# The last tile of every image moved from TensorE's transposes to GpSimd's split and DMA transposes, in a non-local attention kernel

## The reference

```python
g     = (einsum('bchw,oc->bhwo', x, w_g)     + b_g).reshape(B, N, Ci)      # N = 1024, Ci = 64
theta = (einsum('bchw,oc->bhwo', x, w_theta) + b_theta).reshape(B, N, Ci)
phi   = (einsum('bchw,oc->bohw', x, w_phi)   + b_phi[:, None, None]).reshape(B, Ci, N)
att   = softmax(einsum('bnc,bcm->bnm', theta, phi), axis=-1)
y     = einsum('bnm,bmc->bnc', att, g).reshape(B, H, W, Ci)
out   = einsum('bhwc,oc->bohw', y, w_out) + b_out[:, None, None]
inv   = bn_gamma / sqrt(bn_var + 1e-5)
return x + out * inv[:, None, None] + (bn_beta - bn_mean * inv)[:, None, None]
```

## Time and profile before

| | |
|---|---|
| median of 3 runs | 215.8 us (214.25 to 217.01) |
| the profiled execution, time | 214.18 us |
| its span on the core | 212.4 us |
| PE busy | 202.0 us, 95% |
| DVE busy | 181.7 us, 86% |
| ACT busy | 143.4 us, 68% |
| POOL busy | 130.6 us, 61% |
| TensorE clock granted | 1.0 of full speed all through |
| DMA queue of SP | 63.7% of the 16 engines' span |

### The profile page before, as it was taken

One profiled execution on the slowest core, in us unless ns is written; L12 is line 12 of the kernel. 1 busy time (PEld: TensorE's weight loads), 2 busy tenths in 40 slices (PEclk: granted clock), 3 DMA queues, 4 the chain that ended last, 5 costly groups with the idle time before them and its releaser, 6 DMA issues.

```text
span 212.4 us, 4045 instructions
## 1 busy us (share of the span) xinstructions
PE 202.0 (95%) x1156; PEld 137.4 (65%) x1156; DVE 181.7 (86%) x298; ACT 143.4 (68%) x259; POOL 130.6 (61%) x113
## 2 busy tenths in 40 slices
PE   7997969999999999999999999999999999999994
PEld 6685838576665857577575956668575855656542
DVE  0689987987999799977999599977999789989871
ACT  2777857668585848866596666856696585758721
POOL 2449786848489494866679494885769352913400
PEclk9999999999999999999999999999999999999999
DMA  5225991699529974599819994299924994182102
GB/s 159 83 76 109 210 225 27 174 221 238 114 78 241 245 182 99 126 209 250 158 50 218 243 217 113 87 223 251 167 63 105 222 235 104 38 195 49 49 11 91
DMA packets 44716, 31.61 MB, mean 149 GB/s; under 512 B 35616, under 2 KB 36128, under 8 KB 44704
## 3 DMA queue, kind: packets, MB, share of 16 engines
q1 hardware_dynamic: 44416, 31.34, 63.7%
q10 hardware_dynamic: 288, 0.14, 0.2%
HBM read 8.36 MB, written 4.23 MB: 59 GB/s over the span
## 4 chain that ended last, share of the span: by engine, by line
PE 61%; DVE 14%; issue 8%; ACT 6%; DMA 4%; SPq 3%; POOL 2%; ACTq 1%; DVEq 0%
PE ps_scores L713 18%; PE ps_flip L778 13%; PE ps_y L725 10%; PE ps_misc L697 5%; DVE pt_lo L678 5%; PE ps_y L732 5%; DVE neg_max L579 5%; PE ps_misc L803 4%; PE ps_misc L739 4%; ACT probs L537 3%; DVE y_norm L596 2%; DMA phi_ll<-lo 2%; DMA vec<-vectors_dram 2%; SPq L286 2%; ACT pt_hi L525 2%
## 5 line engine op out<-in xcount | busy, mean ns | idle before, releaser
L537 ACT ACTIVATE probs<-ps_scores,neg_max 128x1024 f32<-128x1024 f32 x64 | 71.7, 1121 | 22.5 <-DVE neg_max L579 22.4
L579 DVE TENSOR_REDUCE neg_max<-ps_scores 128x1 f32<-128x1024 f32 x64 | 77.8, 1215 | 1.2 <-PE ps_scores L713 1.2
L678 DVE SCALAR_TENSOR_TENSOR pt_lo<-ps_flip,pt_hi 128x512 f16<-128x512 f32 x98 | 62.9, 684 | 15.3 <-ACT pt_hi L525 15.1
L525 ACT ACTIVATE pt_hi<-ps_flip 128x512 f16<-128x512 f32 x98 | 53.4, 597 | 26.5 <-PE ps_flip L778 26.5
L778 PE MATMUL ps_flip<-ident,probs 128*128 128x128 f32 x392 | 52.7, 276 | 1.1 <-DVE pt_lo L678 0.6
L778 PEld LDWEIGHTS ps_flip<-ident,probs 128*128 128x128 f32 x392 | 43.6, 142 | 13.8 <-issue 6.1
L713 PE MATMUL ps_scores<-phi_hh,theta_hl 128*128 128x512 f32 x128 | 45.7, 438 | 3.8 <-DMA phi_ll<-lo 1.8
L713 PE MATMUL ps_scores<-phi_ll,theta_hl 128*128 128x512 f32 x128 | 40.0, 393 | 0.0
L406 POOL TENSOR_TENSOR p_lo<-probs,p_hi 128x1024 f16<-128x1024 f32 x15 | 32.3, 2155 | 2.9 <-POOL p_hi L402 2.3
L725 PE MATMUL ps_y<-pt_hi,g_parts 128*128 128x512 f16 (+1 forms) x128 | 30.0, 377 | 0.0
L713 PEld LDWEIGHTS ps_scores<-phi_hh,theta_hl 128*128 128x128 f32 x128 | 19.3, 190 | 14.9 <-ACT probs L537 12.2
(11 more groups left out here) (80 smaller groups left out, 179.3 us busy)
## 6 DMA issues: line engine op xcount, KB each, us to landing
x_in<-x_in_dram SPq DMA_DIRECT2D x16, 256.0 KB, 3.2
inv_all<-inv_row SPq DMA_DIRECT2D x15, 256.0 KB, 3.7
out_dram<-resid SPq DMA_DIRECT2D x15, 256.0 KB, 3.1
phi_hh<-hi SPq DMA_DIRECT2D x14, 256.0 KB, 4.9
phi_ll<-lo SPq DMA_DIRECT2D x14, 256.0 KB, 4.1
theta_hl<-hi SPq DMA_DIRECT2D x7, 256.0 KB, 4.0
theta_hl<-lo SPq DMA_DIRECT2D x7, 256.0 KB, 3.8
pt_hi<-p_hi SPq DMA_TRANSPOSE x15, 3.6
```

The lines of the kernel that those rows point to most:

```text
L525: nc.scalar.activation(pt_hi[ring][:, c * HALF_TILES:(c + 1) * HALF_TILES, slot * P:(slot + 1) * P], ps_flip[c][:, :].rearrange("p (a n) - ...
L537: nc.scalar.activation(probs[k % PROB_RING][:, :], ps_scores[k % 2][:, :], ACT.Exp, bias=neg_max[:, k % STEPS:k % STEPS + 1], accum_out=ro ...
L579: nc.vector.tensor_reduce(out=top, in_=ps_scores[k % 2][:, :], op=ALU.max, axis=AX.X, negate=True).then_inc(row_max_ready if by_dma(it, k) ...
L678: nc.vector.scalar_tensor_tensor(out=pt_lo[ring][where], in0=ps_flip[c][:, :].rearrange("p (a n) -> p a n", n=P), scalar=PROB_SCALE, in1=p ...
```

## The change

`BY_DMA` now lists places in an image (0 to 7) and not slots of a half, and place 7 is added: tiles 1, 5 and 7 go by DMA. For that the counts of flips and moves, and the semaphore values that follow from them, are made by image. The buffers `p_hi` and `p_lo` are now one pair for each of the three places (before: one pair for each half). SP's list gets the two transposes of the last tile of the image before, one ahead of the store and one behind it. The last tile of the last image still goes by TensorE, so seven tiles move.

```diff
-    BY_DMA = (1,)
-    BY_PE = tuple(slot for slot in range(HALF_TILES) if slot not in BY_DMA)
-    MOVED = 16 * len(BY_DMA)
+    BY_DMA = (1, 5, 7)
+    BY_PE = tuple(place for place in range(MT) if place not in BY_DMA)
+    IN_HALF = tuple(tuple(place % HALF_TILES for place in BY_DMA if place // HALF_TILES == part)
+                    for part in range(PER_IMAGE))
...
-        p_hi = [[sbuf(f"p_hi{i}{s}", [P, N], F16) for s in BY_DMA] for i in range(2)]
-        p_lo = [[sbuf(f"p_lo{i}{s}", [P, N], F16) for s in BY_DMA] for i in range(2)]
+        p_hi = {place: sbuf(f"p_hi{place}", [P, N], F16) for place in BY_DMA}
+        p_lo = {place: sbuf(f"p_lo{place}", [P, N], F16) for place in BY_DMA}
...
         def by_dma(it, k):
-            return k % HALF_TILES in BY_DMA and not in_last_half(tile_at(it, k))
+            return k % MT in BY_DMA and not in_last_half(tile_at(it, k))
+
+        def counted(it, k, places):
+            before = sum(place < k % MT for place in places)
+            return it * (STEPS // MT * len(places)) + k // MT * len(places) + before
...
+        def moved_each(k):
+            return 16 * len(IN_HALF[ring_of(k)])
 
         def moved_by(it, k):
-            return it * (STEPS // HALF_TILES // 2 * MOVED) + (k // HALF_TILES // 2 + 1) * MOVED
+            return it * (STEPS // MT * moved_each(k)) + (k // MT + 1) * moved_each(k)
...
                 b, r = image_at(it, k), (k // MT) % 2
                 inv_to_row(2 * b - 1)
+                turn_hi(MT * b - 1)
                 store(it, k - 2 * MT + HALF_TILES)
+                turn_lo(MT * b - 1)
                 if exists(b + 2, B):
                     sp.wait_ge(g_ready, b + 1)
                     sp.wait_ge(resid_ready, b + 1)
                     load_x(b + 2, r)
...
                 if exists(t, TILES) and by_dma(it, k - 1):
-                    ring, n = ring_of(k - 1), BY_DMA.index((k - 1) % HALF_TILES)
-                    p, high, low = probs[(k - 1) % PROB_RING], p_hi[ring][n], p_lo[ring][n]
+                    ring = ring_of(k - 1)
+                    p, high, low = probs[(k - 1) % PROB_RING], p_hi[(k - 1) % MT], p_lo[(k - 1) % MT]
                     hold(probs_ready, t + 1)
-                    hold(hi_moved[ring], moved_by(it, k - 1) - MOVED)
+                    hold(hi_moved[ring], moved_by(it, k - 1) - moved_each(k - 1))
```

More of the change, by code:

```diff
@@ L224, in by_dma @@
         def by_dma(it, k):
-            return k % HALF_TILES in BY_DMA and not in_last_half(tile_at(it, k))
+            return k % MT in BY_DMA and not in_last_half(tile_at(it, k))
+        def counted(it, k, places):
+            before = sum(place < k % MT for place in places)
+            return it * (STEPS // MT * len(places)) + k // MT * len(places) + before
         def flip_at(it, k):
             if in_last_half(tile_at(it, k)):
-                return LAST_HALF // HALF_TILES * len(BY_PE) + tile_at(it, k) - LAST_HALF
-            before = sum(slot < k % HALF_TILES for slot in BY_PE)
-            return it * (STEPS // HALF_TILES * len(BY_PE)) + k // HALF_TILES * len(BY_PE) + before
+                return counted(0, LAST_HALF, BY_PE) + tile_at(it, k) - LAST_HALF
+            return counted(it, k, BY_PE)
         def move_at(it, k):
-            before = sum(slot < k % HALF_TILES for slot in BY_DMA)
-            return it * (STEPS // HALF_TILES * len(BY_DMA)) + k // HALF_TILES * len(BY_DMA) + before
+            return counted(it, k, BY_DMA)
+        def moved_each(k):
+            return 16 * len(IN_HALF[ring_of(k)])
         def moved_by(it, k):
-            return it * (STEPS // HALF_TILES // 2 * MOVED) + (k // HALF_TILES // 2 + 1) * MOVED
+            return it * (STEPS // MT * moved_each(k)) + (k // MT + 1) * moved_each(k)
         def ring_of(k):
@@ L289, in turn_hi @@
             def turn_hi(t):
-                if not by_dma(0, t):
+                if t < 0 or not by_dma(0, t):
                     return
@@ L296, in turn_hi @@
                 sp.dma_start_transpose(pt_hi[ring][:, :, slot * P:(slot + 1) * P],
-                                       p_hi[ring][BY_DMA.index(slot)][:, :]).then_inc(hi_moved[ring], 16)
+                                       p_hi[t % MT][:, :]).then_inc(hi_moved[ring], 16)
             def turn_lo(t):
@@ L305, in turn_lo @@
                 sp.dma_start_transpose(pt_lo[ring][:, :, slot * P:(slot + 1) * P],
-                                       p_lo[ring][BY_DMA.index(slot)][:, :]).then_inc(lo_moved[ring], 16)
+                                       p_lo[t % MT][:, :]).then_inc(lo_moved[ring], 16)
             def inv_to_row(h):
@@ L336, in image @@
                     load_x(b + 2, r)
-                turn_hi(MT * b + BY_DMA[0])
+                turn_hi(MT * b + 1)
                 inv_to_all(2 * b - 1)
-                turn_lo(MT * b + BY_DMA[0])
+                turn_lo(MT * b + 1)
                 if exists(b + 1, B):
@@ L352, in image @@
                 inv_to_all(2 * b)
-                turn_hi(MT * b + HALF_TILES + BY_DMA[0])
-                turn_lo(MT * b + HALF_TILES + BY_DMA[0])
+                turn_hi(MT * b + HALF_TILES + 1)
+                turn_lo(MT * b + HALF_TILES + 1)
             for it in range(B // 2):
@@ L404, in step @@
                     hold(p_hi_ready, move_at(it, k - 1) + 1)
-                    hold(lo_moved[ring], moved_by(it, k - 1) - MOVED)
+                    hold(lo_moved[ring], moved_by(it, k - 1) - moved_each(k - 1))
                     nc.gpsimd.tensor_tensor(low[:, :], p[:, :], high[:, :],
@@ L520, in step @@
                     slot, ring = (k - 2) % HALF_TILES, (k - 2) // HALF_TILES % 2
-                    if slot in (0, BY_PE[0]):
+                    if slot == 0:
                         wait(act, y_ready, half_at(it, k - 2) - 1)
@@ L621, in step @@
                         dve.wait_ge(inv_raw_ready, half_at(it, k - 1) + 1)
-                        moved = inv_sum[:, cols.start + BY_DMA[0]:cols.start + BY_DMA[-1] + 1:2]
+                        slots = IN_HALF[ring_of(k - 1)]
+                        moved = inv_sum[:, cols.start + slots[0]:cols.start + slots[-1] + 1:2]
                         nc.vector.tensor_scalar(out=moved, in0=moved, scalar1=PROB_SCALE, scalar2=None,
```

## The result

The changed kernel takes 222.6 us (median of 4 runs, 222.2 to 223.4), the kernel before 216.4 in the same runs: the ratio is 1.033, 95% interval 1.026 to 1.039. It is slower. The profiled execution took 222.62 us, its span is 220.8; against the profiled execution of before that is 8.4 us, against the medians 6.2. The difference between the two is told further down. Medians here are of all executions, and the ratios leave out those that took over 1.5% longer than the fastest of the same kernel.

The account below looks back on a forecast made before the run. TensorE was taken as nearly always busy, its scores waiting for ACT's probabilities or the restack DMAs. Stalls of 7.5 us less a gain of 2.9 gave +4.6 us, forecast 220.0 us (217.5 to 223; with other cases 212.5 to 224).

Parts of the forecast that it names:

- Which chain decides: Scores of the next tile 0 wait for the last restack DMA in six images, 7.5 us in all (6.3 to 10.8).
- The shift by GpSimd's split: Split of tile 7 queued ahead of g_parts shifts g_parts by 2.4 us and resid by 2.1 us.
- The shift by the store: Store behind tile 7's high transpose holds resid 0.3 us beyond GpSimd's shift; rival with 1.4 us: up to +9 us, chance 0.12.
- The restack chain's length: From the end of tile 1's low split to the last restack's landing: 11.3 us, unchanged by a later start.
- The argument against a backlog of the DMA engines: Two images show equal chains with and without x's load; against the rival that the restack absorbs the shift, -2.9 us, chance 0.16.
- Halving the stall: At next tile 0's scores, a stall s makes the next 2.5 - s; alternating or settling at half, mean 1.25 us (1.05 to 1.8).
- The gain: Step 1, scores of tile 2 start 0.42 us earlier, limited by ACT's probabilities of tile 0; seven images, 2.9 us.
- the slack: Time the restack has to spare at the next tile 0's scores: 0.5 us in one image, none in another; taken as 0.3.

Follow-up runs that it names:

- turn of order: GpSimd makes hi and lo before splitting tile 1; SP issues all six restacks ahead of tile 1's transposes, store and inv_row. Kernel before so turned: 213.7 us, ratio 0.989.
- split alone: Changed kernel with GpSimd's split of tile 7 kept but its two DMA transposes left out, late first TensorE instruction: ratio 1.020 to the kernel before.
- the transposes alone: Changed kernel with GpSimd splitting only 16 columns of tile 7 and both DMA transposes kept in full: 219.5 us, ratio 1.016 to the kernel before.
- the restack first: Changed kernel, all its work kept, with the turn of order on GpSimd and SP: 212.8 us, ratio 0.983 to the kernel before.
- the repeat: The changed kernel run again with no edit: 222.9 us, ratio 1.030 to the kernel before.
- without tile 7: Tile 7 neither transposed, split nor moved (its slot holds zeros), with the turn of order: 211.4 us, ratio 0.976 to the kernel before.
- without any of the cost: Changed kernel in its original order, tile 7 neither transposed, split nor moved, TensorE's first wait removed: 215.5 us, ratio 0.994 to the kernel before.
- the exchange of lo: Kernel before with lo's three restack DMAs ahead of the store and inv_row in SP's list: 216.0 us, ratio 0.997 to the kernel before.

## Why the prediction came out right, and what was off

**The number: near, and in part by luck.** I said 220.0 us (217.5 to 223), it is 222.6. Of the 2.6 us between them 0.6 is the kernel before, which was 216.4 in these runs and not 215.8, and 2.0 is the change: +6.2 and not +4.2. The largest chance of mine, 0.51, was on no difference beyond 2%, and slower by over 2% had 0.43. In the sum a missing cost (the clock, the first image) and gains that were a little larger than forecast partly cancel; they are set out below.

**Which chain decides: right.** Six images have scores that wait for the last restack, as forecast, 8.2 us in all against a forecast of 7.5 (6.3 to 10.8). The turn of order that keeps every instruction and takes nearly all of that wait away brings 10 us, 3.3 of which the kernel before gains by it too. This is shown.

**The shift by GpSimd's split: right in mechanism.** The split of tile 7 ends 3.8 us after ACT's end on that tile (forecast 109.3 - 105.34 = 4.0), and `g_parts` is released by the queue, as it should be. In image 3, whose predecessor had hardly a stall, `g_parts` starts 2.1 us later behind the scores of tile 0 than before (6.90 and 4.78 us), where I had 2.4. The split alone has 7.4 us of stalls in its profile. The time of that run, burdened with a late start, is too uncertain to size it.

**The shift by the store: right on average, wrong in the worst image.** I gave it 0.3 us beyond GpSimd's shift, at most 1.4. It is nothing in four of the six images, 0.40 in one, and in one 2.2 us:

```profile
93.56 1.12 POOL L456 TENSOR_SCALAR resid<-x_in,bn 128x1024 f32<-128x1024 f32 x1 [2.19 <-DMA out_dram<-resid]
```

In that image SP took 3.02 us to issue one transpose and could issue the store only then:

```profile
87.87 3.02 SPq L302 DMA_TRANSPOSE pt_hi<-p_hi  x1
90.95 0.56 SPq L289 DMA_DIRECT2D out_dram<-resid  x1
```

What I had missed is the issue itself: I took 1.24 us for it from the earlier trace rows. I also took it for a part that matters only behind GpSimd's; with the transposes alone `resid` waits 6.6 us for the store. The occupation of the DMA engines, for which I had an upper bound of 1.9 us a transpose, comes out at 1.7 by the queue's shares.

**The restack chain's length: too short.** I carried 11.3 us over unchanged. That was the shortest of six images: in the profile of before the chain takes 11.3 to 12.0 us, 11.6 on average, and in that of the changed kernel 11.6 to 12.3, 11.9 on average. In image 3, which has the worst stall, it is 12.3 and was 11.4: SP's issues up to the first `phi_ll` take 7.1 and not 6.5 us, and the landing of the second 4.6 and not 4.3. The argument against a backlog of the DMA engines was half wrong: with the restack first, the `phi_ll` issues begin at 118.0 and 119.0, the next scores start at 125.85, and the DMAs take 6.8 us to land, where they took 4.1. The row of that kernel's trace:

```profile
L292 SPq DMA_DIRECT2D phi_ll<-lo x2: 597/734/872, 118.0 to 119.0; - x2
...
DMA to landing us min/median/max: 6.8/6.8/6.8
```

So an earlier issue gives back a good part of what it wins, as it did with the restack of lo ahead of the store, and only because the turn moved it so far did it suffice. No run shows what stretches the landings.

**Halving the stall: there, and hidden once by the store.** I expected stalls that alternate or settle at half of 2.5 us. They are 0.32, 3.23, 1.70, 1.04, 1.39 and 0.57, in the repeat nearly the same, with a mean of 1.37 against my 1.25. The 3.23 comes behind a stall of only 0.32, so it has the full shift. Counted from the scores of the image's tile 0 the last restack lands 3.15 us later than in the same image before, TensorE is ready 0.39 sooner, and there was 0.37 of slack. Behind those 3.23 us the split of tile 7 costs nothing, as the argument says, for `g_parts` waits for DVE again:

```profile
88.69 0.69 POOL L418 TENSOR_SCALAR g_parts<-g_raw,g_factor 128x512 f16<-128x512 f32 x1 [1.70 <-DVE g_factor L663]
```

The next stall is 1.70 all the same, because in that image the store is 2.19 us late (above). Then the stalls stay near 1. With the transposes left out they alternate: 0.02, 3.20, 0.58, 2.14, 0 and 1.44, and `g_parts` waits 2.74 and 0.66 us for DVE behind the two large ones and not at all behind the small ones. That is one profile, with dips of the clock in it.

**The gain: right where it arises, and smaller in sum.** Step 1 of the kernel after, TensorE (the scores of tile 1, then of tile 2) and ACT between them:

```profile
59.84 0.71 PE L722 MATMUL ps_scores<-phi_hh,theta_hl 128*128 128x512 f32 x2
...
61.92 0.73 PE L722 MATMUL ps_scores<-phi_hh,theta_hl 128*128 128x512 f32 x2
```

```profile
61.65 0.21 ACT L545 ACTIVATION_READ_ACCUMULATOR probs<-ps_scores,neg_max 128x1 f32 x1
```

The scores of tile 2 start at 61.92, 0.06 after ACT's 61.86: the limit that I named. The distance is 2.08 us against 2.50 in the earlier trace rows (108.59 - 106.09), 0.42 less. With the restack out of the way seven images bring 2.3 us and not 2.9. In the two profiles, both with the restack first and no stall behind the first image, step 1 gains 3.4 us in the seven images, and 1.2 us come back between the scores of tile 0 and those of tile 1 (3.86 us in three of the images without tile 7, 3.68 in the same three of the kernel before). DVE's small operation of 0.15 us ahead of the probabilities of tile 7 would fit; it wasn't tried alone. And in the original order not all of the gain was there to have: without any of the cost it was 1.4 us (0.3 to 2.5 by the interval), because the restack had no more slack to give. My sum had the slack in it as 0.3 us, but none of the 3.6 us of stalls that this run has.

**The term that was missing: the clock.** The prediction has none for it. After two of the stalls TensorE runs at the lower clock for a few microseconds. From the scores of tile 0 to those of tile 1 it is 3.66 to 3.67 us in five images of the changed kernel, behind stalls of 0.3 to 1.7 us, but 5.26 from 83.16 on and 5.35 from 30.59 on, where the windows show 0.52 and 0.62: 1.6 to 1.7 us each. Those 3.3 us and 1.0 more of stall in the first image are the largest parts of what the profiled difference of 8.4 us has beyond my 4.6.

The same term would explain why the profiled execution of before (214.18, clock 1.0) lies below its median. Of the executions of the kernel before in the batch with the exchange of lo, those at a mean clock of 1.0 took 214.4 to 216.3 us, and seven of the nine at 0.991 and 0.992 took 216.6 to 217.5. The kernel before with that exchange, profiled at a mean clock of 0.992, has one dip, in the first image, and takes 5.32 us from the scores of tile 0 to those of tile 1 there, where the profile of before has 3.67. So it is likely, though no trace of the kernel before itself shows it, that this kernel often pays one such dip too, and that the difference of the medians, 6.2 us, is smaller than that of the profiles for that reason.

**The sum.** For the profiled executions: stalls +8.0, first image +1.0, scores of tile 0 to those of tile 1 +2.3 (two dips, together 3.3, less 1.0 us in the images where before it is 4.0 to 4.1 us and after 3.7), step 1 -3.2 (2.08 against 2.49 to 2.65 us, seven times), and 0.3 that I can't place: 8.4. Forecast: +7.5 and -2.9.

## What to carry to other kernels

Before work is moved to an idle engine, follow that engine's next instructions: GpSimd was 39% idle, but the split stood in front of the one series of operations that led, over a hand-ordered DMA queue, to a wait of the busy engine which had 0 to 0.6 us of slack. Moving the same work cost 6 us in one order and gained 1 in the other, each against a kernel before in the same order, and the better order by itself was worth 3 us to the kernel before. So the order is to be settled first: what the busiest engine will wait for goes to the front of each queue that it passes, ahead of work whose reader comes later. And a stall of the tensor engine is to be priced above its length, since the clock may drop behind it.

## What the runs showed of the hardware that I had not expected

- TensorE's granted clock fell to 0.5 to 0.6 for some 3 us right after an idle stretch of 3 us at the scores (80 to 83 us: busy 0.07 of 3.00, then clock 0.52), and after a wait in the first image. Behind stalls of 0.3 to 1.7 us in the same execution it didn't fall. Each dip cost 1.6 to 1.7 us beyond the stall. The length of the wait alone doesn't decide it: in the first image TensorE stood idle for 1.8 us both in the profile of before, where the clock stayed at 1.0, and in that with the exchange of lo, where it fell to 0.57, and in the repeat of the changed kernel it stood idle for 2.4 us there and the clock stayed.
- SP's issue of a DMA transpose took 1.23 to 1.36 us in all 30 of the kernel before. In the changed kernel 7 of 44 took 1.6 us or more, the longest 3.02 (from 87.8 to 91.0 us, with the DMA engines at 0.85). With the restack first 8 of the 22 transposes of a high part took 2.1 to 3.1 us.
- The landing of an SBUF copy of the same size (`phi_ll`) went from 4.1 to 6.8 us with the restack first, when it was issued earlier, among the load of x and the other restacks.
